# First self attention: one head at a time from memory, or two heads at a time from the projection's own tiles

## The chip, the cores and the metric

The program runs on one core of one Trainium2 chip, as one launch. The metric is device time in microseconds. TensorE multiplies matrices into PSUM, ScalarE evaluates functions, VectorE and GpSimd do elementwise work and reductions, SyncE only issues DMAs here. The engines run side by side and wait for each other through semaphores. Each engine takes its instructions in program order.

## The reference

Four layers of attention and feed-forward work on x (2 batches of 1024 tokens of 256). The change concerns the first attention alone:

```
q = l2norm(layer_norm(x) @ Wq) * q_scale            # 8 heads of 64
k, v = split(concat([layer_norm(x), layer_norm(ctx)]) @ Wkv); k = l2norm(k) * k_scale
sim = q . k * 8, masked where a context key is barred (keys 1024 to 1100)
out = softmax(sim) @ v
x = x + layer_norm(out @ Wo)
```

So there are 16 pairs of batch and head (B = 2, 8 heads), 1024 queries and 1101 keys each. The other stages (mixture of experts, two cross attentions, a second self attention, an fp4 feed-forward) are the same before and after.

## The kernel before

A stage is a block of code with buffers of its own; the next begins when all engines have ended. The first attention has three stages after its layer norm.

`project_normed` (stage qkv0) computes rows of q and k in 34 jobs: fp32 products into PSUM, squares on ScalarE, sums on VectorE, division by the length, transposition by TensorE, and a scaled copy into qT and kT, where two heads of 64 lie above each other in the 128 partitions. It ends with v (18 jobs). SyncE stores qT, kT and a row of mask values to device memory.

`head_attention` (stage heads0) takes 16 heads one after the other. BUFS = 4 sets of buffers are loaded from memory by SyncE (`load`, L1233 to L1257). For a head:
- `peak`: TensorE computes scores in bf16, queries in the partitions, 128 queries against 1101 keys (three products, L1307); VectorE takes the maximum of each query (`take_max`, L1420). Eight of these a head.
- `turn_max` (L1314), `copy_max` (L1431), `load_max` (L1263): the eight columns of maxima are transposed, copied and laid by DMA as row 64 of q, against a row of ones in k; row 65 holds the mask. This is done LEAD - 1 = 1 head ahead.
- `score` (L1332): 18 units (9 chunks of 128 keys by 2 halves of 512 queries), keys in the partitions, fp32, so that the maximum is taken off inside the product. ScalarE makes the exponential (L1408).
- `value` (L1344): the weighted sum of v, two chunks side by side in column tiles of 64.
- `add_weights` (L1458, VectorE) adds the nine chunks of exponentials; `fold` (L1320) transposes sums and weights, VectorE reduces (L1469, L1439) and multiplies by the inverse (L1446).

Which use of the shared PSUM comes after which score is written out by hand in USES and TIMES. The heads 4 to 11 run in a hardware loop, the first and last four are straight code. The PE order in a unit is score, value of an earlier group, and then what TIMES lists:

```
def score(n, u, i, j):
    ...
    pe.matmul(score_ps[0:rows, i % RING, :], k[:, u, c * P:c * P + rows], q[:, u, x:x + spec.unit],
              start=True, stop=True).then_inc(score_done, 1)
```

`output_rows` (stage out0, L1785 to L1875) packs the heads on GpSimd, transposes them (L1820), multiplies by Wo (L1808), and then normalises: one root over all 16 tiles after the last one, and whole-tile operations on VectorE.

`quad_attention`, the second self attention, is not changed. It already works with four heads of 16 at a time, with row tiles for the maximum rounds (L1638), fp32r scores (L1660) and column tiles for the sums (L1669). The cross attentions use row tiles of 32 with fp32 (L523).

Of the kernel before, what the change touches and what calls it, by code (L numbers as in the profile page):

```python
# [1096 lines left out]
def head_attention(nc, core, name, spec, q_dram, k_dram, mask_dram, values, out):  # L1097
# [5 lines left out]

    N, NU, HW, KEYS, QU = spec.n, spec.units, spec.width, spec.keys, spec.q_units
    W1 = HW + 1  # L1110
    BUFS, LEAD, LAG = 4, 2, 2
    SIDES = 4 if W1 <= 32 else 2
    SIDE = P // SIDES
    APART = SIDE < W1
    VW = HW if APART else W1
    ADDS = spec.chunks - 1
    GROUP = SIDES * QU
    GROUPS = -(-NU // GROUP)
    RING = 2 if spec.split else 3
    PROBS = 12 if APART else NU  # L1120
    assert BUFS * NU % PROBS == 0 and PROBS % QU == 0

    VALUE_TIMES = [list(range(QU))] if APART else [[x] for x in range(QU)]
    KEY_BANKS = -(-KEYS // 512)
    SHARED = 2 if KEY_BANKS == 2 else 1
    ROWS = 2 if spec.split else 1
    LOADS = 6 if spec.split else 5
    CF = KEYS // P

    TURN, FOLD, WEIGHTS = "turn", "fold", "weights"
    USES = [0, 1, TURN, 2] + ([WEIGHTS] if APART else []) + [3, FOLD] + list(range(4, BT))


    TIMES = [0, 2, 4, 5, 7, 9, 10, 12, 14, 16, 17] if APART else [0, 1, 3, 4, 6, 7, 9, 11, 12, 14]
    use_at = {k: [] for k in range(NU)}
    for time, x in zip(TIMES, USES, strict=True):
        use_at[time].append(x)
    assert SHARED == 1 or len(USES) % SHARED == 0  # L1140

    def exists(n, use):
        head = n + {TURN: LEAD - 1, FOLD: -1, WEIGHTS: -1}.get(use, LEAD)
        return 0 <= head < N

    uses_before, count = {}, LEAD * BT + LEAD - 1
    for n in range(N):
        for x in USES:
            uses_before[n, x] = count
            count += exists(n, x)  # L1150
    steady = uses_before[1, USES[0]] - len(USES)
    assert uses_before[N // 2, FOLD] == steady + len(USES) * (N // 2) + USES.index(FOLD)

    def before(n, use):

        return uses_before[n, use] if isinstance(n, int) else steady + len(USES) * n + USES.index(use)

    def buffer(n, use):
        return (uses_before[n, use] if isinstance(n, int) else steady + USES.index(use)) % SHARED

    with Stage(nc, name) as st:
        q = st.sb("q", [P, BUFS, S], spec.dtype)
        k = st.sb("k", [P, BUFS, KEYS], spec.dtype)
        narrow = not spec.split
        if narrow:
            q_peak = st.sb("q_peak", [P, BUFS, S], BF16)
            k_peak = st.sb("k_peak", [P, BUFS, KEYS], BF16)
        head_values = st.sb("head_values", [P, BUFS, spec.chunks, SIDE])
        minus_max = st.sb("minus_max", [P, BUFS, BT])
        max_rows = st.sb("max_rows", [BT, BUFS, ROWS, P], spec.dtype)  # L1170
        probs = st.sb("probs", [P, PROBS, spec.unit])
        sums = st.sb("sums", [P, 2, S])
        folded = st.sb("folded", [P, BT, VW])
        if APART:
            weights = st.sb("weights", [P, 2, S])
            added = st.sem("added")
        rsum = st.sb("rsum", [P, BT])
        shared_ps = st.ps("shared_ps", [P, SHARED, KEY_BANKS, 512])
        score_ps = st.ps("score_ps", [P, RING, spec.unit])
        sums_ps = st.ps("sums_ps", [P, S])  # L1180

        peaks = [shared_ps[:, x, :, :].rearrange("p a b -> p (a b)") for x in range(SHARED)]

        early = [peaks[0], score_ps[:].rearrange("p a b -> p (a b)")] if SHARED == 1 else peaks
        turned = [shared_ps[:, x, 0:2, :].rearrange("p a (t c) -> p a t c", t=4) for x in range(SHARED)]

        loaded = [st.sem(f"loaded{u}") for u in range(BUFS)]
        max_loaded = [st.sem(f"max_loaded{u}") for u in range(BUFS)]
        cleared, keys_cleared, narrowed = st.sem("cleared"), st.sem("keys_cleared"), st.sem("narrowed")
        shared_done, shared_read = st.sem("shared_done"), st.sem("shared_read")  # L1190
        high_done, max_ready = st.sem("high_done"), st.sem("max_ready")
        score_done, exp_done, value_done = st.sem("score_done"), st.sem("exp_done"), st.sem("value_done")
        sums_copied = st.sem("sums_copied")
        rsum_done, normed = st.sem("rsum_done"), st.sem("normed")
        n_keys_cleared = 4 if narrow else 2
        block = st.block()

        def at_least(eng, sem, value):

            if not (isinstance(value, int) and value <= 0):  # L1200
                eng.wait_ge(sem, value)

        def heads(eng, body):

            last = N // BUFS - 1
            for u in range(BUFS):
                body(u, u, 0)
            with eng.Fori(1, last) as j:
                for u in range(BUFS):
                    body(BUFS * j + u, u, j)  # L1210
            for u in range(BUFS):
                body(BUFS * last + u, u, last)

        def slot(u, i):

            return (NU * u + i) % PROBS

        def groups_upto(n, i):

            return GROUPS * n + i // GROUP + 1 if i >= 0 else GROUPS * (n - 1) + (i + NU) // GROUP + 1  # L1220

        def adds_upto(n, i):

            return ADDS * n + max(i // QU, 1) if i >= 0 else ADDS * (n - 1) + max((i + NU) // QU, 1)

        def beyond(n, ahead):

            return isinstance(n, int) and not 0 <= n + ahead < N

        @block.sync  # L1230
        def _(sp):
            def load(n, u):
                sp.dma_start(head_values[:, u, 0:CF, 0:VW].unsqueeze(1),  # L1233
                             values[:, bass.ds(n, 1), 0:CF, 0:VW]).then_inc(loaded[u], 16)
                if CF < spec.chunks:
                    rows = KEYS - CF * P
                    sp.dma_start(head_values[0:rows, u, CF:CF + 1, 0:VW].unsqueeze(1),
                                 values[0:rows, bass.ds(n, 1), CF:CF + 1, 0:VW]).then_inc(loaded[u], 16)
                if spec.split:

                    row = spec.peak_row
                    sp.dma_start(q[row:row + ROWS, u, :].bitcast(F32),
                                 q[row + ROWS:row + 2 * ROWS, u, :].bitcast(F32)).then_inc(loaded[u], 16)

                    for part in range(2):
                        src = q_dram[part, bass.ds(n, 1), :, :]
                        sp.dma_start(q[2 * part * HW:2 * (part + 1) * HW, u, :].bitcast(F32),
                                     src.to_broadcast([2, HW, S])).then_inc(loaded[u], 16)
                    for r in range(2):
                        src = k_dram[:, bass.ds(n, 1), :, :].rearrange("a o w s -> a (o w) s")  # L1250
                        sp.dma_start(k[2 * r * HW:2 * (r + 1) * HW, u, :].bitcast(F32), src).then_inc(loaded[u], 16)
                else:
                    sp.dma_start(q[0:HW, u, :], q_dram[0, bass.ds(n, 1), :, :].rearrange(
                        "o w s -> (o w) s")).then_inc(loaded[u], 16)
                    sp.dma_start(k[0:HW, u, :], k_dram[0, bass.ds(n, 1), :, :].rearrange(
                        "o w s -> (o w) s")).then_inc(loaded[u], 16)
                    sp.dma_start(k[HW:HW + 1, u, :], mask_dram[bass.ds(n, 1), :]).then_inc(loaded[u], 16)  # L1257

            def load_max(n, u):
                sp.wait_ge(max_ready, n + 1)  # L1260
                for r in range(ROWS):
                    row = spec.peak_row + r
                    sp.dma_start(q[row:row + 1, u, :].bitcast(F32),  # L1263
                                 max_rows[:, u, r, :].bitcast(F32)).then_inc(max_loaded[u], 16)

            sp.wait_ge(cleared, 3)
            sp.wait_ge(keys_cleared, n_keys_cleared)
            for n in range(BUFS):
                load(n, n)
            for n in range(LEAD - 1):  # L1270
                load_max(n, n)

            def body(n, u, j):
                if not beyond(n, LEAD - 1):
                    load_max(n + LEAD - 1, (u + LEAD - 1) % BUFS)
                if not beyond(n, BUFS - 1) and not beyond(n, -1):
                    sp.wait_ge(value_done, GROUPS * n)
                    load(n + BUFS - 1, (u - 1) % BUFS)

            heads(sp, body)  # L1280

# [1764 lines left out]
```

## Time and profile before

| | us |
|---|---|
| three runs, median (lowest to highest) | 3163.11 (3160.62 to 3172.48) |
| profiled execution, its own time | 3165.68 |
| span of its instructions | 3163.9 |

| engine | busy us, share of the span |
|---|---|
| TensorE (PE) | 2409.5, 76% |
| weight loads (PEld) | 1401.1, 44% |
| VectorE (DVE) | 1544.5, 49% |
| ScalarE (ACT) | 1126.9, 36% |
| GpSimd (POOL) | 347.7, 11% |

The shares are means over stages that have different limits, so the stages have to be looked at one by one. An fp32 product of the program stands as two matmul records. A busy TensorE says that records cover the time, not that it runs at its best speed: the granted clock (PEclk) stands beside it, 1.00 for 2.4 GHz and 0.50 for 1.2 GHz.

### The profile page before, as it was taken

What the parts mean: (1) busy time and instruction counts of PE and PEld (TensorE: products, weight loads), DVE (VectorE), ACT (ScalarE), POOL (GpSimd) and SP (SyncE); (2) the same over time, 40 slices, a digit from 0 to 9 for tenths busy, and PEclk for the clock granted to TensorE, in tenths of its full rate; (3) what the DMA queues carried; (4) which work ended last, traced back from release to release, by engine and by line L of the source; (5) the groups of instructions that cost most, each with busy time, mean ns of one, the idle gap of its engine ahead of it and who ended that gap; (6) DMA issues with size and microseconds to landing.
All of it is one profiled execution on the core that took longest, in us unless ns stands there. A gap on an engine that the chain in (4) does not pass through costs nothing. (4 is left out here: it accounts for less than half of the span.)

```text
span 3163.9 us, 38714 instructions
## 1 busy us (share of the span) xinstructions
PE 2409.5 (76%) x12273; PEld 1401.1 (44%) x12274; DVE 1544.5 (49%) x2425; ACT 1126.9 (36%) x2389; POOL 347.7 (11%) x369
## 2 busy tenths in 40 slices
PE   4959999998227587679999729996865999484487
PEld 2413333335117444323333319995333999331254
DVE  4657777763652354667786150002344000347665
ACT  3403333333103235126667424442432444233211
POOL 0010000001004201300000002221001222102211
PEclk9969999999558788759999959998786999686599
DMA  1220010100106300613342146663024666200001
GB/s 55 90 64 22 22 32 21 25 7 11 53 0 203 96 1 19 141 13 45 37 55 28 37 136 213 198 199 124 16 89 144 197 200 198 84 1 28 7 13 33
DMA packets 156570, 233.95 MB, mean 74 GB/s; under 512 B 48758, under 2 KB 110770, under 8 KB 156450
## 3 DMA queue, kind: packets, MB, share of 16 engines
q1 hardware_dynamic: 146754, 205.91, 23.8%
q0 software_dynamic: 9696, 26.49, 2.2%
q8 instruction: 69, 1.13, 0.2%
q14 instruction: 51, 0.42, 0.0%
HBM read 186.56 MB, written 38.86 MB: 71 GB/s over the span
## 5 line engine op out<-in xcount | busy, mean ns | idle before, releaser
L1721 DVE TENSOR_REDUCE heads_part_max<-heads_shared_ps 128x2 f32<-128x1024 f32 x256 | 300.0, 1220 | 90.1 <-PE heads_shared_ps L1638 90.1
L2759 PE MATMUL experts_up_ps<-experts_rowT,experts_w 128*128 128x128 f32 x2864 | 341.0, 277 | 0.0
L1705 ACT ACTIVATE heads_probs<-heads_score_ps 128x512 f32<-128x512 f32 x512 | 266.4, 602 | 191.0 <-PE heads_score_ps L1660 191.0
L2759 PEld LDWEIGHTS experts_up_ps<-experts_rowT,experts_w 128*128 128x128 f32 x2864 | 333.0, 194 | 0.2
L1408 ACT ACTIVATE heads_probs<-heads_score_ps 128x512 f32<-128x512 f32 (+1 forms) x288 | 171.9, 598 | 382.1 <-PE heads_score_ps L1332 380.3
L2909 DVE TENSOR_TENSOR experts_y<-experts_down_ps,experts_b_now 128x256 f32<-128x256 f32 x78 | 33.1, 425 | 555.6 <-PE experts_down_ps L2769 555.6
L1332 PE MATMUL heads_score_ps<-heads_q,heads_k 128*128 128x512 f32 (+1 forms) x576 | 291.6, 616 | 0.3 <-DVE heads_minus_max L1420 0.3
L2819 ACT ACTIVATE experts_hT<-experts_up_ps,experts_b_now 128x128 f32<-128x128 f32 x624 | 222.6, 368 | 46.5 <-PE experts_up_ps L2759 9.8
L1660 PE MATMUL heads_score_ps<-heads_q,heads_k 66*128 66x512 f32 x512 | 198.0, 474 | 29.5 <-ACT heads_probs L1705 25.3
L1420 DVE TENSOR_REDUCE heads_minus_max<-heads_shared_ps 128x1 f32<-128x1101 f32 x120 | 155.9, 1299 | 113.5 <-PE heads_shared_ps L1307 113.4
L2769 PE MATMUL experts_down_ps<-moe_w,experts_hT 128*128 x808 | 184.4, 379 | 0.0
L1660 PEld LDWEIGHTS heads_score_ps<-heads_q,heads_k 66*128 66x128 f32 x512 | 92.2, 201 | 198.4 <-ACT heads_probs L1705 163.5
L2769 PEld LDWEIGHTS experts_down_ps<-moe_w,experts_hT 128*128 128x128 f32 x808 | 148.9, 190 | 17.8
L1344 PE MATMUL heads_sums_ps<-heads_probs,heads_head_values 128*64 128x512 f32 (+1 forms) x576 | 154.6, 605 | 0.0
L1669 PE MATMUL heads_sums_ps<-heads_probs,self_values 128*32 128x512 f32 x1024 | 146.8, 647 | 4.1 <-ACT heads_sums L1697 4.1
L2708 POOL DMA_INDIRECT y_dram<-experts_y,experts_index x101 | 99.4, 985 | 454.3 <-DVE experts_y L2909 410.4
L2769 PE MATMUL experts_down_ps<-l1f_w,experts_hT 128*128 x624 | 141.0, 379 | 0.0
L1458 DVE TENSOR_TENSOR heads_weights<-heads_probs,heads_weights 128x1024 f32<-128x1024 f32 (+1 forms) x112 | 136.2, 1216 | 6.4 <-ACT heads_probs L1408 5.2
L1332 PEld LDWEIGHTS heads_score_ps<-heads_q,heads_k 128*128 128x128 f32 (+1 forms) x576 | 92.1, 187 | 92.4 <-issue 71.5
L2800 ACT ACTIVATE experts_rowT<-experts_rowT_ps 128x256 f32<-128x256 f32 x62 | 23.8, 384 | 296.4 <-PE experts_rowT_ps L2749 296.3
L2769 PEld LDWEIGHTS experts_down_ps<-l1f_w,experts_hT 128*128 128x128 f32 x624 | 115.7, 190 | 14.1
L1307 PE MATMUL heads_shared_ps<-heads_k_peak,heads_q_peak 128*128 128x512 bf16 x360 | 80.9, 335 | 40.7 <-DVE heads_k_peak L1480 26.0
(556 smaller groups left out, 3370.3 us busy)
## 6 DMA issues: line engine op xcount, KB each, us to landing
experts_w<-in_L_ffn_W SPq DMA_DIRECT2D x39, 1024.0 KB, 5.2
experts_w<-in_L_ffn_w SPq DMA_DIRECT2D x39, 1024.0 KB, 5.1
heads_q<-l_queries SPq DMA_DIRECT2D x48, 256.0 KB, 12.1
experts_w<-in_L_ffn_W SPq DMA_DIRECT2D x23, 512.0 KB, 3.9
core_xT<-y_dram SPq DMA_DIRECT2D x20, 512.0 KB, 4.7
experts_b_now<-in_L_ffn_b SPq DMA_DIRECT2D x78, 128.0 KB, 2.9
heads_k<-l_keys SPq DMA_DIRECT2D x32, 256.0 KB, 14.0
l1f_w<-in_L_ffn_W SPq DMA_DIRECT2D x8, 1024.0 KB, 11.9
```

The lines of the kernel that those rows point to most:

```text
L1332: pe.matmul(score_ps[0:rows, i % RING, :], k[:, u, c * P:c * P + rows], q[:, u, x:x + spec.unit], start=True, stop=True).then_inc(score_do ...
L1344: done = pe.matmul(sums_ps[x * SIDE:(x + 1) * SIDE, part * spec.unit:(part + 1) * spec.unit], head_values[0:rows, u, c, :], probs[0:rows, ...
L1408: act.activation(probs[0:rows, slot(u, i), :], score_ps[0:rows, i % RING, :], ACT.Exp, scale=spec.scale).then_inc(exp_done, 1)
L1420: dve.tensor_reduce(minus_max[:, u, s:s + 1], src[:, 0:KEYS], AX.X, ALU.max, negate=True).then_inc(shared_read, 1)
L1458: dve.tensor_tensor(total, chunk_probs(u, c)[0:rows, :], chunk_probs(u, 0) if c == 1 else total, ALU.add).then_inc(added, 1)
L1660: pe.matmul(score_ps[:, i % RING, :], k[:, u, r, c * P:(c + 1) * P], q[:, u, r, half * 512:(half + 1) * 512], start=True, stop=True).then_ ...
L1669: done = pe.matmul(sums_ps[r * SIDE:(r + 1) * SIDE, :], values[:, n, c, :], probs[:, t % SLOTS_OF_PROBS, r, :], start=(c == 0), stop=(c == ...
L1705: act.activation(probs[:, t % SLOTS_OF_PROBS, r, :], score_ps[:, i % RING, :], ACT.Exp, scale=SC).then_inc(exp_done, 1)
L1721: dve.tensor_reduce(part_max[:, g % 2, 2 * pair:2 * pair + 2, s, x], two, AX.X, ALU.max).then_inc(shared_read, 1)
L2759: done = pe.matmul(up_ps[:, f % 4, 0:SLOT], w1_sb[:, u, c, f * P:(f + 1) * P], rowT[:, u % 2, c, :], start=(c == 0), stop=(c == DC - 1))
L2769: done = pe.matmul(down_ps[:, u % 2, 0:D], hT[:, u % 2, f, :], second.sb[:, bass.ds(e, 1), f, :].rearrange("p o d -> p (o d)"), start=(f = ...
L2819: act.activation(hT[:, u % 2, f, :], up_ps[:, f % 4, 0:SLOT], func, bias=bias).then_inc(act_done, 1)
```

## The change

`head_attention` is replaced by `pair_attention`, `output_rows` by `output_normed` for this stage, and `project_normed` keeps its results on the chip.

- qT and kT stay in SBUF. GpSimd makes bf16 copies (q16, k16) during the projection. No store to memory, no loads of heads. Barred context keys are replaced in k16 by key 0 (six VectorE operations at the end of the projection), and the mask is the bias of the last chunk's exponential.
- A pair is the two heads of one 128-partition tile: 8 pairs, 18 steps each (2 halves by 9 chunks). A step's scores are two fp32 products of 64 rows, in row tiles 0 and 64, into two banks. Ahead of them two fp32r products of ones2 with max_rows put the negated maximum (as a high and a low part, two rows a head) into the same banks. One exponential covers both heads (1024 columns).
- Maximum rounds are a third of the keys (367 columns) of one head, in row tiles, three banks in a ring, three rounds in each step but steps 3 and 12. 48 rounds belong to a pair; 48 + 9 are done before the first step.
- The weights are added by VectorE (chunks 0, 2, 4, 8) and GpSimd (1, 3, 5, 6, 7) into two totals, merged by VectorE in the second step after the half. TensorE sums over the partitions by a product with ones (steps 3 and 12). SyncE lays the sums over 128 partitions, VectorE inverts them, SyncE stores and spreads them, and GpSimd scales the result in qT.
- Everything is straight code.
- `output_normed` needs no packing and no transposes; ScalarE copies the rows out, and statistics, roots and the last operations go in groups of four tiles; GpSimd adds the bias to x.

```
+    SLOTS_OF_PROBS, BANKS = 5, 3
+    BY_POOL = [1, 3, 5, 6, 7]
+    BY_VECTOR = [0, 2, 4, CHUNKS - 1]
+    NO_UNITS, TURN_AT, WEIGH_AT = (3, 12), 15, {3: 1, 12: 0}
+    LEAD = 9
...
+    work_at[-1] = units[0:UNITS] + [(TURN, 0)] + units[UNITS:UNITS + LEAD]
...
+        if s not in NO_UNITS and t < STEPS:
+            work_at[t] += left[0:3]
...
+            def load_max(g):                      # SyncE
+                sp.wait_ge(max_ready, g + 1)
+                for r in range(2):
+                    for part in range(2):
+                        row = HW * r + part
+                        sp.dma_start(max_rows[row:row + 1, g % 2, :].bitcast(F32),
+                                     max_parts[r * BT:(r + 1) * BT, part, :].bitcast(F32)).then_inc(max_loaded[g % 2], 16)
+            def invert(w):
+                sp.wait_ge(weights_copied, w + 1)
+                for r in range(2):
+                    sp.dma_start(compact[:, v, r, :], weights[HW * r:HW * r + 1, :]).then_inc(compact_loaded, 16)
+                sp.wait_ge(inverted, w + 1)
...
+                sp.dma_start(weights_dram[v, :, :]..., inverse[:, v, :, :]).then_inc(stored, 16)
+                sp.wait_ge(stored, 16 * (w + 1))
...
+                for r in range(2):
+                    sp.dma_start(spread[HW * r:HW * (r + 1), v, :], ...).then_inc(spread_loaded[v], 16)
+            for t in range(-1, STEPS + 4):
+                for item in work_at[t]:
+                    if item[0] == TURN:
+                        load_max(item[1])
+                    elif item[0] == WEIGH:
+                        invert(item[1])
...
+            def score(t):                         # TensorE
+                if t % PER == 0:
+                    pe.wait_ge(max_loaded[g % 2], 64 * (g // 2 + 1))
+                if t >= 2:
+                    pe.wait_ge(exp_done, t - 1)
+                for r in range(2):
+                    of = slice(HW * r, HW * (r + 1))
+                    pe.matmul(score_ps[0:rows, t % 2, r, :], ones2[of, 0:rows], max_rows[of, g % 2, half * 512:(half + 1) * 512],
+                              start=True, stop=False, tile_position=(HW * r, 0))
+                for r in range(2):
+                    of = slice(HW * r, HW * (r + 1))
+                    done = pe.matmul(score_ps[0:rows, t % 2, r, :], kT[of, c, b, chunk * P:chunk * P + rows],
+                                     qT[of, c, queries(t)[1]], start=False, stop=True, tile_position=(HW * r, 0))
+                done.then_inc(score_done, 1)
...
+            for t in range(STEPS):
+                score(t)
+                for item in work_at[t]:
+                    share(item)
+                if t:
+                    value(t - 1)
...
+            for t in range(STEPS + 4):            # VectorE
+                for item in work_at[t]:
+                    if item[0] != WEIGH:
+                        take(item)
+                if 1 <= t <= STEPS and (t - 1) % CHUNKS in BY_VECTOR[1:]:
+                    add(t - 1)
+                w = t // CHUNKS - 1
+                if t % CHUNKS == 2 and 0 <= w:
+                    merge(w)
+                if t % CHUNKS == 6 and 0 <= w and t < STEPS:
+                    invert(w)
+            invert(HALVES * PAIRS - 1)
```

`share` waits until the bank's last reader is done (`free`) and then makes a maximum round, the transposition of the maxima (TURN), or the product with ones (WEIGH). `value` makes two products of 64 columns, one a head, in column tiles. GpSimd takes its adds as the exponentials come, and `scale(w)` in the step of chunk 7 of the next half.

## Rows read from the trace of the kernel before

**Rows 1.** Windows: stretch; length, busy us (instructions) by engine; clock, DMA share, GB/s.
```profile
core 0: us, PE busy (x) PEld busy (x) DVE busy (x) ACT busy (x) POOL busy (x), PEclk, DMA share, GB/s
...
226.00:231.00 5.00, 4.86 (x8) 1.98 (x9) 2.51 (x2) 0.68 (x2) 0.00 (x0) 0.53 0.00 0
231.00:236.00 5.00, 5.00 (x18) 1.85 (x18) 1.58 (x2) 2.90 (x5) 0.00 (x0) 1.00 0.02 4
300.00:700.00 400.00, 388.70 (x1370) 144.35 (x1366) 288.16 (x276) 140.39 (x231) 0.00 (x0) 1.00 0.10 23
...
1376.00:1434.00 58.00, 58.00 (x200) 18.30 (x200) 30.02 (x27) 27.50 (x53) 0.00 (x0) 0.50 0.00 1
```

**Rows 2.** Timeline of SyncE's queue, one period: start us, us, engine, line.
```profile
397.60 0.72 SPq L1263 DMA_DIRECT2D heads_q<-heads_max_rows  x1
...
430.62 0.73 SPq L1263 DMA_DIRECT2D heads_q<-heads_max_rows  x1
```

**Rows 3.** Groups by line, 190 to 749 us: count, busy us, mean ns, idle before.
```profile
L1332 PE MATMUL heads_score_ps<-heads_q,heads_k 128*128 128x512 f32 (+1 forms) x576 | 291.6, 616 | 0.3 <-DVE heads_minus_max L1420 0.3
...
L1420 DVE TENSOR_REDUCE heads_minus_max<-heads_shared_ps 128x1 f32<-128x1101 f32 x120 | 155.9, 1299 | 113.5 <-PE heads_shared_ps L1307 113.4
L1344 PE MATMUL heads_sums_ps<-heads_probs,heads_head_values 128*64 128x512 f32 (+1 forms) x576 | 154.6, 605 | 0.0
L1458 DVE TENSOR_TENSOR heads_weights<-heads_probs,heads_weights 128x1024 f32<-128x1024 f32 (+1 forms) x112 | 136.2, 1216 | 6.4 <-ACT heads_probs L1408 5.2
...
L1320 PE MATMUL heads_shared_ps<-core_ident,heads_sums 128*128 128x128 f32 x128 | 17.2, 277 | 7.9 <-DVE heads_minus_max L1420 6.5 <-DVE heads_rsum L1469 1.4
```

**Rows 4.** Timeline of the output stage.
```profile
753.57 1.97 PE L1820 MATMUL out_turned_ps<-core_ident,out_packed 128*128 128x128 f32 x8 [6.94 <-DMA out_bias<-in_L_xattn_ln_o_b]
...
755.37 3.78 PE L1808 MATMUL out_row_ps<-out_w,out_headsT 128*128 128x256 f32 x8
...
808.54 4.42 DVE L1875 TENSOR_TENSOR core_x<-core_x,out_rows 128x4096 f32<-128x4096 f32 x1
```

**Rows 5.** Timeline at the seams of the three stages.
```profile
171.69 0.69 DVE L2194 COPY self_values<-qkv_v_ps 77x512 f32<-77x512 f32 x1 [1.03 <-PE qkv_v_ps L2101]
...
226.14 2.05 PE L1332 MATMUL heads_score_ps<-heads_q,heads_k 128*128 128x512 f32 x2 [0.28 <-DVE heads_minus_max L1420]
...
747.97 0.69 DVE L1446 TENSOR_TENSOR self_heads_out<-heads_folded,heads_rsum 128x512 f32<-128x512 f32 x1
...
749.15 0.44 SPq L1785 DMA_DIRECT2D out_w<-in_L_xattn_Wo  x1
```

**Rows 6.** The page's costliest groups: the second self attention's maximum.
```profile
L1721 DVE TENSOR_REDUCE heads_part_max<-heads_shared_ps 128x2 f32<-128x1024 f32 x256 | 300.0, 1220 | 90.1 <-PE heads_shared_ps L1638 90.1
```

**Rows 7.** Line L1613, the second self attention's loads of maximum rows.
```profile
DMA to landing us min/median/max: 2.1/2.1/2.2
```

**Rows 8.** Timeline of TensorE, tiled products of a cross attention and the second self attention.
```profile
2291.80 1.93 PE L523 MATMUL x_banks<-x_qT,x_k_half 32*77 32x512 f32 x8
2293.66 0.63 PE L529 MATMUL x_banks<-x_barredT,x_bar 77*77 77x512 bf16 x2
...
1507.10 0.49 PE L1660 MATMUL heads_score_ps<-heads_q,heads_k 66*128 66x512 f32 x1 [0.22 <-ACT heads_probs L1705]
1507.52 0.40 PE L1638 MATMUL heads_shared_ps<-self_k_narrow,self_q_narrow 32*128 32x512 bf16 x4
1507.85 1.06 PE L1669 MATMUL heads_sums_ps<-heads_probs,self_values 128*32 128x512 f32 x8
1508.84 0.96 PE L1660 MATMUL heads_score_ps<-heads_q,heads_k 66*128 66x512 f32 x3
```

**Rows 9.** The fp4 stage: timeline, then line L2246 with ns min/median/max.
```profile
2927.97 3.47 POOL L2241 TENSOR_TENSOR fp4w_rows_x<-fp4w_rows_x,fp4w_rows_power 128x1024 f32<-128x1024 f32 x1
2929.28 3.51 DVE L2246 TENSOR_TENSOR fp4w_raw<-fp4w_wide_x,fp4w_wide_scale 128x1280 f32<-128x1280 f32 x1
...
L2246 POOL TENSOR_TENSOR ffn_rows<-fp4w_rows_x,fp4w_rows_scale x4: 1930/2162/3059, 2913.5 to 2939.6; 128x1024 f32<-128x1024 f32 x4
L2246 DVE TENSOR_TENSOR fp4w_raw<-fp4w_wide_x,fp4w_wide_scale x2: 1492/2502/3511, 2929.3 to 2952.0; 128x1280 f32<-128x1280 f32 x2
```

More of the change, by code:

```diff
@@ L1230, in _ @@
         @block.sync
         def _(sp):
[L1232 to L1243, printed above, removed]
-                    for part in range(2):
[L1246 to L1271, printed above, removed]
@@ new lines, in scale @@
+            def scale(w):
+                v = w % 2
+                c, to = queries(w * CHUNKS)
+                pool.wait_ge(spread_loaded[v], 32 * (w // 2 + 1))
+                pool.wait_ge(sums_copied, w + 1)
+                pool.tensor_tensor(qT[:, c, to], qT[:, c, to], spread[:, v, :], ALU.mult).then_inc(scaled, 1)
+            for t in range(STEPS):
+                g, half, c = parts(t)
+                if c in BY_POOL[1:]:
+                    add(t)
+                if c == 7 and t >= CHUNKS:
+                    scale(t // CHUNKS - 1)
@@ L1386, in _, with free @@
-            heads(pe, body)
-            value(N - 1, BUFS - 1, GROUPS - 1, range(QU))
-            if APART:
-                pe.wait_ge(added, ADDS * N)
-                fold(weights, (BUFS - 1) % 2, count, 0)
-            pe.wait_ge(sums_copied, N)
-            fold(sums, (BUFS - 1) % 2, count + APART, (count + APART) % SHARED)
+            def free(used):
+                if used >= BANKS:
+                    reader, n = reads[used - BANKS]
+                    pe.wait_ge(weights_copied if reader == "scalar" else shared_read, n)
@@ new lines, in value @@
+            def value(t):
+                g, half, chunk = parts(t)
+                b, c = place(g)
+                rows = spec.chunk_rows(chunk)
+                pe.wait_ge(exp_done, t + 1)
+                if chunk == 0 and t:
+                    pe.wait_ge(sums_copied, t // CHUNKS)
+                for r in range(2):
+                    done = pe.matmul(sums_ps[HW * r:HW * (r + 1), :], values[0:rows, b * spec.heads + 2 * c + r, chunk, :],
+                                     probs[0:rows, t % SLOTS_OF_PROBS, r, :], start=(chunk == 0), stop=(chunk == CHUNKS - 1),
+                                     tile_position=(0, HW * r))
+                done.then_inc(value_done, 1)
```

675 lines of the change are left out of this document (349 added, 326 removed).

## The prediction

> **What bounds the kernel now.** I read the windows first. In the steady part of the first self attention (300 to 700 us) TensorE is busy 389 of 400 us at a granted clock of 1.00, its 2.4 GHz level, VectorE 288, ScalarE 140 [rows 1]. So this stage is TensorE's. The period of one head stands in SyncE's issues of the maximum row: 397.60 and 430.62, 33.0 us [rows 2], 16 heads, 528 us. The grouped lines say what fills it: score (L1332), weighted sum (L1344) and transposes (L1320) are fp32 products, while VectorE's maximum (L1420) and adding of weights (L1458) leave slack [rows 3]. One fp32 product of 512 columns costs 0.86 us at 2.4 GHz (four of 256 columns took 3.8 us at half clock, 0.45 each at full [rows 4]); a head has 18 for scores (15.5 us), 9 pairs for sums (7.7; two column tiles share one time), 16 transposes (2.1), 8 bf16 rounds for the maximum (3.7): 29 of 33 us. Ahead of the loop, VectorE's last copy of the projection starts at 171.69, the first score at 226.14; behind it lies a tail to 748.7, then an output stage from 749.15 to 813.0 [rows 4, 5].
>
> **Projection and start.** V's products keep TensorE busy to about 171, so the removed stores of q and k were covered and gain nothing. Added: six VectorE operations of 308 elements for the padded keys, some 0.46 us each with waits about 3.2 us, uncovered; two small mask loads, 0.5. GpSimd's bf16 copies lie beside TensorE. Then the clearing of big buffers, the loading of heads and the narrowing go (171.7+0.7 to about 198). New prologue: 1.8 us for max_rows and 0.8 for the ones; 57 reductions of 367 columns. A reduction costs 1.3 us for 1101 columns, 1.22 for 1024 [rows 3, 6]: 1.03 ns a column and 0.15 fixed, 0.55 us for 367, 0.51 apart when they queue (an estimate: they end up to 0.04 closer than they last). 48 x 0.51 = 24.5, reduce, transpose and two copies 1.9, four row loads: 4 x 0.72 issue, 2.1 to landing [rows 2, 7], 4.3 behind the first wait. The stage starts at 176.5, so the first score comes at 176.5 + 2.6 + 24.5 + 1.9 + 4.3 = 209.8, say 210.5 instead of 226.1: 15.6 gained. Bounds: 10 (SyncE late) to 20.
>
> **One step of the new loop** (two heads, one chunk, 512 queries; 18 steps a pair, 8 pairs), at 2.4 GHz.
> - Maximum by a product: 2 fp32r products side by side. Three fp32r products took 0.96 us, one 0.49: 0.235 apart [rows 8]. With the weight load 0.30.
> - Score: two fp32 products of 64 rows in row tiles. The nearest row is the mask attention's: four products of 32 rows in two pairs went from 2291.80 to 2293.66, 0.93 a pair, switch included [rows 8]. I take 0.88. If they don't overlap: 1.73.
> - Maximum rounds: three of 367 bf16 columns, 0.15 each by a column a cycle, neighbours in different row tiles; four tiles of 512 took 0.33 where one after another would be 0.85 [rows 8]. I take 0.31; 0.46 apart.
> - Sum: two column tiles, 0.86, plus 0.11 and 0.14 for the two changes of tile shape (0.33 for 0.21, 0.99 for 0.85 [rows 8]).
> Sum 2.6 us. A pair: 16 x 2.6 + 2 x 2.3 (steps without rounds) = 46.2, two ones products with waits for the merge 2 x 1.6 = 3.2, transpose 0.3: 49.7.
> VectorE a pair: 48 x 0.51 + 8 adds x 1.22 [rows 3] + small ones 2.2 = 36.5, below TensorE. ScalarE has the same exponentials as now, 140 us in 12.1 heads [rows 1], so 23. GpSimd 8 adds x 1.93 [rows 9] + 2 scalings = 17.6.
> Adding on two engines is not free. In the fp4 stage a GpSimd add of 1024 elements took 3.47 us where its fastest took 1.93, and the VectorE one beside it 3.51 instead of 1.49 [rows 9]: each waited the other out. Here VectorE's adds of chunks 2 and 4 come up about 3.1 us into their step, when GpSimd has just begun (2.7) on chunk 3 or 5: 1.5 us of waiting, 4 times a pair, VectorE 42.5. That still lies under TensorE, but a bank comes free late after chunk 4; I add 0.9 a pair: 50.6. From below 0, from above 8 full waits of 1.93, VectorE 52 with the rounds at 0.55, 54, so 3.4 more a pair.
> The Trainium skill (SBUF — State Buffer, "SBUF: two separate sides") says that the shared port pair is "an exclusive lock, not a bandwidth split", taken by a VectorE operation with two SBUF inputs only against a GpSimd operation that reads SBUF. The trace agrees on the lock, 3.51 against 1.49 [rows 9]. By that rule the reductions from PSUM are free of it; if it struck them too, 17.6 us of GpSimd would stand beside 24.5 of reductions, VectorE would reach some 50, and the time would be that of the second rival below.
>
> **The seam between pairs.** The first score of a pair waits for four loads of maximum rows. Their copy is placed in step 15, three steps or 7.8 us ahead. But in that step SyncE's queue still holds the inversion of the last weights: it waits for VectorE's reciprocal (behind three reductions and two copies, 4.3 us into step 15), stores (2.1 us to landing [rows 7]), waits for it, issues two spreads (1.5), and only then the four rows (2.2 to the last issue, 2.1 to landing). 4.3 + 0.1 + 2.1 + 0.1 + 1.5 + 2.2 + 2.1 + 0.2 = 12.6; 12.9 with half of a late add. TensorE stands still 5.1 us, and in order: rounds and the last sum are queued behind that score. Then the clock: it was at 0.50 when the old loop began, 0.53 over the first 5 us, 1.00 after [rows 1]. I charge 2.6 us a seam (about 5 us at half speed). 7 x 7.7 = 54. Bounds 0 and 7 x 10. 2.5 more for the loop's own start at half clock.
> Loop: 8 x 50.6 + 54 + 2.5 = 461.3, end at 671.8.
> Tail after the last exponential, all in a row: add and merge 2.6, ones product 1.3, copy 0.6, compaction 2.9, reciprocal 0.3, store 2.3, spread 3.8, scaling 1.0, with hand-overs 15.5 to 16.5. Stage ends at 688, before 748.7: 60.7 gained in all up to here.
>
> **Output stage.** Same load before the first product (749.15 to 753.57), then no transposes: 64 products of 256 columns x 0.43 = 27.5, half clock at the start 2.5 (the old one shows 3.78 for eight records [rows 4]), then of the last group copy, statistics, root, inverse and eight operations of 256, 5.5. 4.4 + 30 + 5.5 = 40 against 63.8: 23.5 gained (bounds 18 to 27). The whole-tile operations of 4.4 us at the old end, last at 808.54 [rows 4], are taken apart into groups beneath TensorE.
>
> Sum: 60.7 + 23.5 = 84. Later stages are untouched. The profiled span is 3163.9, its own time 3165.7, 2.6 above the median 3163.1. Median forecast 3163 - 84 = 3079.
>
> **Rivals.**
> 1. The seam is covered (landings quicker, or steps long enough that three of them last 12 us at no other cost): the 54 us go, 3025. For: SyncE's own waits are short when nothing is queued. Against: the order on SyncE is fixed and each landing is 2.1 us. 0.15.
> 2. The two adding engines bind: every VectorE add waits a whole GpSimd add. 8 x 3.4 = 27 more, with jitter 35: 3110. For: [rows 9]. Against: 45% load of GpSimd. 0.15.
> 3. The other side: row tiles of 64 rows with fp32 weights run one after the other. Place: score of each step; price 0.06 + 0.85 + 0.15, with the maximum product 0.24 more, 1.24 a step x 144 = 179; three steps then last 11.5 us, so the seam gives back 7 x 6.4 = 45: 3079 + 134 = 3213. It decides from 0.6 us a step (84 / 144). Against: rows of 32 do overlap [rows 8]. 0.05.
> 4. The clock stays at half. The later quad attention began with light rounds, then TensorE was busy 58 of 58 us at 0.50 [rows 1]. Against: its products fill 66 rows and 32 columns, the old loop's full ones brought 1.00 in 5 us, and here two tiles fill the array again. Throughout it would cost 2.2 us x 144 less the seams, 260: 3340; for the first pair alone, 20. 0.05 for the whole.
> Forecast 0.60, its own range 3050 to 3110.
>
> A measurement of this kernel tells about 0.5% (16 us) from no change. Faster: forecast, rivals 1 and 2, 0.90; same 0.02; slower 0.08 (rivals 3 and 4 less their mild forms, and mishaps). The range that leaves out at most 2 in 10: 3018 to 3150.
>
> **What would show it.** Score records of both heads starting within 0.1 us and a step of 2.6 us (else rival 3); a TensorE gap of 4 to 6 us before each pair's first score, ended by a DMA of max_rows, and clock 0.5 behind it (else rival 1); VectorE adds of 1.2 and of 2.5 to 3 us in the same loop; first score near 210; output stage of 40 us. Wrong would be: pair period far from 58 us, or windows of the loop at 0.5.

## The result, and the profile after

The changed kernel took 3027.3 us (median of 4, 3022.5 to 3037.7), the kernel before 3161.9 in runs beside it (3142.4 to 3172.5): ratio 0.959, 95% interval 0.953 to 0.964. That is 134.5 us where 84 were forecast: inside the range of 3018 to 3150, below the likeliest case's own range (3050 to 3110), and within 3 us of the time of rival 1 (3025). The profiled execution took 3037.7, span 3035.7; it answers to the 3165.7 of before, so the traces differ by 128 us. Where each stage stands in them, from views of the same kind:

| us | before | forecast | after |
|---|---|---|---|
| first score | 226.1 | 210.5 | 206.5 |
| first score to the end of the last exponential | | 461.3 | 428.8 |
| first score to stage end | 522.5 | 477.5 | 445.2 |
| output stage | 63.8 | 40 | 40.1 |
| SyncE's first moe_w load of the stage behind | 814.3 | | 693.6 |
| the remainder of the kernel (to the span's end) | 2349.6 | as before | 2342.1 |

120.7 us had been won when the stage behind the output begins. The other 7.5 are a matter of later stages, told of in the point on them below. (The profiled execution was the slowest of its four, so its 128 us lie under the 134.5 of the medians. In the second trace of the changed kernel, below, the remainder is 2330.1, 12 us shorter: later stages differ by that much between two executions of one kernel.)

The windows answer to [rows 1]: a plain stretch of the loop, then the seam between the first and the second pair in three pieces, then the last pair, and last the start of the second self attention.

```profile
core 0: us, PE busy (x) PEld busy (x) DVE busy (x) ACT busy (x) POOL busy (x), PEclk, DMA share, GB/s
240.00:249.70 9.70, 9.40 (x47) 3.00 (x43) 6.06 (x10) 3.89 (x5) 4.08 (x2) 1.00 0.02 2
249.70:251.90 2.20, 0.04 (x1) 0.00 (x0) 2.20 (x3) 0.81 (x1) 1.94 (x2) 1.00 0.00 0
251.90:256.40 4.50, 4.48 (x16) 1.40 (x16) 1.61 (x6) 0.23 (x1) 1.72 (x1) 0.62 0.03 1
256.40:261.00 4.60, 4.30 (x22) 1.39 (x23) 2.78 (x6) 1.91 (x2) 3.59 (x2) 1.00 0.32 61
1252.70:1267.70 15.00, 15.00 (x55) 4.79 (x53) 7.91 (x7) 8.15 (x16) 0.00 (x0) 0.50 0.00 1
```

TensorE's gap is 2.2 us, VectorE is busy all through it, and the granted clock behind it is 0.62. That is a mean of the two levels: the clock stands at 0.50, its 1.2 GHz level, for 3.4 of the 4.5 us (252.5 to 255.9) and at 1.00 for the rest. The timeline of the same seam (start, us, engine, line; in brackets the idle time before and who ended it) says who it was. First TensorE, step 15 of pair 0 from 248.08, then VectorE, then GpSimd, then SyncE.

```profile
248.08 0.50 PE L1295 MATMUL heads_score_ps<-heads_max_rows,heads_ones 64*128 64x512 f32 x2
248.41 1.02 PE L1299 MATMUL heads_score_ps<-self_qT,self_kT 64*128 64x512 f32 x4
249.27 0.47 PE L1272 MATMUL heads_shared_ps<-self_k,self_q 64*128 64x367 bf16 x3
251.92 0.28 PE L1276 MATMUL heads_shared_ps<-core_ident,heads_minus_max 128*16 128x128 f32 x1 [2.17 <-DVE heads_part_max L1382]
252.12 1.60 PE L1311 MATMUL heads_sums_ps<-heads_probs,self_values 128*64 128x512 f32 x4
...
254.25 1.87 PE L1299 MATMUL heads_score_ps<-self_qT,self_kT 64*128 64x512 f32 x4
...
260.31 0.50 PE L1295 MATMUL heads_score_ps<-heads_max_rows,heads_ones 64*128 64x512 f32 x2 [0.30 <-DMA heads_max_rows<-heads_max_parts]
```

```profile
248.49 0.20 DVE L1387 TENSOR_REDUCE heads_minus_max<-heads_part_max 128x16 f32<-128x48 f32 x1
248.61 2.80 DVE L1418 TENSOR_TENSOR core_xT<-core_xT,heads_probs 128x1024 f32<-128x1024 f32 x1
251.33 1.42 DVE L1382 TENSOR_REDUCE heads_part_max<-heads_shared_ps 128x1 f32<-128x367 f32 x3
```

```profile
247.98 2.35 POOL L1238 TENSOR_TENSOR core_xT<-core_xT,heads_probs 128x1024 f32<-128x1024 f32 x1 [3.76 <-ACT heads_probs L1363]
250.59 3.03 POOL L1238 TENSOR_TENSOR core_xT<-core_xT,heads_probs 128x1024 f32<-128x1024 f32 x1 [0.26 <-ACT heads_probs L1363]
```

```profile
253.63 0.40 SPq L1205 DMA_DIRECT2D heads_inverse_rows<-heads_inverse  x1
255.22 1.12 SPq L1210 DMA_DIRECT2D heads_spread<-heads_inverse_rows  x2
256.38 2.75 SPq L1194 DMA_DIRECT2D heads_max_rows<-heads_max_parts  x4
```

Read together: the three rounds of step 15 fill the three banks. VectorE can't empty one, for its add of chunk 4 started at 248.61, inside GpSimd's add of 247.98 to 250.33, and lasted 2.80 instead of 1.22. So the transpose, which needs a bank, goes 2.17 us late. Only then does SyncE's chain run, as the prediction has it; it ends with a wait of 0.30 us at the first score.

The groups by line over the loop (206 to 636 us) answer to [rows 3]: idle time before a group, with who ended it, is the last column.

```profile
L1295 PE MATMUL heads_score_ps<-heads_max_rows,heads_ones 64*128 64x512 f32 x256 | 67.4, 521 | 11.4 <-DMA heads_max_rows<-heads_max_parts 11.4
...
L1281 PE MATMUL heads_shared_ps<-core_xT,heads_ones 128*64 128x512 f32 x60 | 16.2, 611 | 3.8 <-DVE core_xT L1424 3.8
...
L1276 PE MATMUL heads_shared_ps<-core_ident,heads_minus_max 128*16 128x128 f32 x7 | 1.9, 277 | 13.0 <-DVE heads_part_max L1382 13.0
```

```profile
L1382 DVE TENSOR_REDUCE heads_part_max<-heads_shared_ps 128x1 f32<-128x367 f32 x329 | 156.5, 531 | 127.5 <-PE heads_shared_ps L1272 127.1
L1418 DVE TENSOR_TENSOR core_xT<-core_xT,heads_probs 128x1024 f32<-128x1024 f32 x16 | 43.4, 2715 | 8.4 <-ACT heads_probs L1363 8.4
...
L1418 DVE TENSOR_TENSOR core_xT<-heads_probs 128x1024 f32<-128x1024 f32 x16 | 19.5, 1220 | 12.2 <-ACT heads_probs L1363 12.2
```

The output stage, against [rows 4]: the products of line 1726, and the last group's last operations.

```profile
656.65 30.59 PE L1726 MATMUL out_row_ps<-out_w,self_qT 128*128 128x256 f32 x128 [15.41 <-DMA out_scale<-in_L_xattn_ln_o_w]
...
690.55 1.67 DVE L1771 SCALAR_TENSOR_TENSOR core_x<-out_rows,out_std,core_x 128x256 f32<-128x256 f32 x4
```

### The profile page after: what moved, and what is told of

Same layout as the page of the kernel before. It is cut to its first block and busy times, and to the rows that moved or that the text cites. A ratio compares the mean times of both kernels' runs of the same rounds, so it can differ in the third digit from the quotient of the medians.

```text
span 3035.7 us, 38003 instructions
## 1 busy us (share of the span) xinstructions
PE 2299.9 (76%) x12297; PEld 1336.9 (44%) x12298; DVE 1425.4 (47%) x2551; ACT 1093.3 (36%) x2264; POOL 542.5 (18%) x467
## 5 line engine op out<-in xcount | busy, mean ns | idle before, releaser
L1382 DVE TENSOR_REDUCE heads_part_max<-heads_shared_ps 128x1 f32<-128x367 f32 x384 | 181.1, 530 | 128.3 <-PE heads_shared_ps L1272 127.8
L2859 ACT ACTIVATE experts_hT<-experts_up_ps,experts_b_now 128x128 f32<-128x128 f32 x624 | 208.1, 367 | 83.0 <-PE experts_up_ps L2799 66.0
L1586 PE MATMUL heads_score_ps<-heads_q,heads_k 66*128 66x512 f32 x512 | 190.5, 455 | 31.5 <-ACT heads_probs L1631 27.3
L1363 ACT ACTIVATE heads_probs<-heads_score_ps 128x1024 f32<-128x1024 f32 x128 | 131.1, 1024 | 218.2 <-PE heads_score_ps L1299 215.7
L1311 PE MATMUL heads_sums_ps<-heads_probs,self_values 128*64 128x512 f32 (+1 forms) x576 | 158.9, 629 | 0.2 <-ACT heads_probs L1360 0.2
L1299 PE MATMUL heads_score_ps<-self_qT,self_kT 64*128 64x512 f32 (+1 forms) x576 | 155.9, 620 | 0.0
L1595 PE MATMUL heads_sums_ps<-heads_probs,self_values 128*32 128x512 f32 x1024 | 138.9, 615 | 4.3 <-ACT heads_sums L1623 4.3
L1238 POOL TENSOR_TENSOR core_xT<-core_xT,heads_probs 128x1024 f32<-128x1024 f32 x48 | 122.6, 2554 | 82.6 <-ACT heads_probs L1363 80.6
L2742 POOL DMA_INDIRECT experts_row<-rows_dram,experts_index x101 | 99.0, 980 | 81.1 <-DVE experts_index L2940 46.2
```

The costliest lines, as they stand in the source:

```text
L1238: pool.tensor_tensor(total, first, probs[:, t % SLOTS_OF_PROBS, :, :], ALU.add).then_inc(pool_added, 1)
L1299: done = pe.matmul(score_ps[0:rows, t % 2, r, :], kT[of, c, b, chunk * P:chunk * P + rows], qT[of, c, queries(t)[1]], start=False, stop=Tr ...
L1311: done = pe.matmul(sums_ps[HW * r:HW * (r + 1), :], values[0:rows, b * spec.heads + 2 * c + r, chunk, :], probs[0:rows, t % SLOTS_OF_PROBS ...
L1363: act.activation(probs[:, t % SLOTS_OF_PROBS, :, :], score_ps[:, t % 2, :, :], ACT.Exp, scale=SC).then_inc(exp_done, 1)
L1382: dve.tensor_reduce(part_max[:, g % 2, r, s, x:x + 1], bank[:, 0:PIECE], AX.X, ALU.max).then_inc(shared_read, 1)
L1586: pe.matmul(score_ps[:, i % RING, :], k[:, u, r, c * P:(c + 1) * P], q[:, u, r, half * 512:(half + 1) * 512], start=True, stop=True).then_ ...
```

## The experiments

Lines of the diffs are of `pair_attention`. "Loop" is from the first score to the end of the last exponential (the changed kernel's first trace: 428.8 us). First a control.

> The changed kernel once more, unedited, so that the edits beside it are compared with it on the same chip. Both theories: 3022 to 3038 us, the loop's first score to the last exponential 429 us, each of the seven seams between pairs 4 to 9 us over the plain steps.

Measured: 3027.3 us, loop 429.7, six seams like the first, one of 9 us. So a loop's length repeats to about 1 us between the two traces, and the kernel's median to 0.1 us.

**VectorE alone adds.**

```diff
-    BY_POOL = [1, 3, 5, 6, 7]
-    BY_VECTOR = [0, 2, 4, CHUNKS - 1]
+    BY_POOL = []
+    BY_VECTOR = list(range(CHUNKS))
...
-                if t % CHUNKS == 2 and 0 <= w:
-                    merge(w)
```

> VectorE adds all nine chunks of weights, GpSimd only scales; the merge goes. Theory A (the seam's stall stands at the transpose, which waits for a bank that VectorE gives back late because its add waited for GpSimd's): every add lasts 1.22 us, the gap before the transpose falls from 2.2 to below 1 us, the clock holds at the seams, loop 400 to 410 us instead of 429, kernel 20 to 28 us below the changed one. Theory B (the seam's stall is the row loads behind SyncE's inversion): the gap only moves to the first score and the clock still falls, loop within 8 us of 429. Rival to both (VectorE becomes the bound: 48 reductions 21.5 us, 16 adds 19.5, small ones 2 of a pair of 49.5, and 2.7 us in a step of 2.6): steps of 2.7 to 2.9 us, loop above 435.

Measured: 3033.3 us, ratio to before 0.960 (0.955 to 0.966), loop 428.3: no faster than the changed kernel, as theory B had forecast, and theory A's 400 to 410 failed. (The four runs lie at 3022.7, 3023.5, 3043.2 and 3044.0; the trace is the first.) The adds last 1.22 us, none waits for GpSimd. The wait at the transposes fell from 13.0 to 3.5 us, and the wait for the loads rose from 11.4 to 25.4. By line over the loop, then one seam:

```profile
L1295 PE MATMUL heads_score_ps<-heads_max_rows,heads_ones 64*128 64x512 f32 (+1 forms) x288 | 74.3, 511 | 25.4 <-DMA heads_max_rows<-heads_max_parts 25.4
...
L1276 PE MATMUL heads_shared_ps<-core_ident,heads_minus_max 128*16 128x128 f32 x7 | 1.9, 277 | 3.5 <-DVE heads_part_max L1382 3.5
```

```profile
254.19 1.08 PE L1311 MATMUL heads_sums_ps<-heads_probs,self_values 128*64 128x512 f32 x4
258.42 0.80 PE L1295 MATMUL heads_score_ps<-heads_max_rows,heads_ones 64*128 64x512 f32 x2 [3.15 <-DMA heads_max_rows<-heads_max_parts]
```

This seam is the one that was forecast: a gap before the pair's first score, ended by the DMA of the rows, at full clock until then. In the changed kernel it was hidden behind the wait at the transpose. VectorE as the bound is refuted too: steps of 2.61.

**GpSimd alone adds**, and the ones products read its sum.

```diff
-    BY_POOL = [1, 3, 5, 6, 7]
-    BY_VECTOR = [0, 2, 4, CHUNKS - 1]
+    BY_POOL = list(range(CHUNKS))
+    BY_VECTOR = []
...
-                if t % CHUNKS == 2 and 0 <= w:
-                    merge(w)
```

> GpSimd adds all nine chunks, VectorE only takes maxima; the merge goes. Theory A: VectorE is idle when a bank fills, so no wait at the transpose, no fall of the clock there, GpSimd at 8 x 2.36 + 1.27 = 20.1 us a half of 24.7; loop 400 to 405, kernel 25 to 30 us below the changed one. Theory B: loop within 8 us of 429, since SyncE's order is unchanged. Rival: GpSimd binds, because an add of 2.36 us in a step of 2.6 leaves no room for the scaling (1.3): probabilities' slots come free late once a half, loop above 435.

Measured: 3012.3 us, 0.952 (0.947 to 0.956), loop 415.6, 13 less than the changed kernel: about half of theory A's figure, and more than theory B's 8. The waits are 2.9 us at the transposes and 17.3 for the loads. Its adds last 2.34 to 2.38 us, none longer for VectorE, and it does not bind: steps stay at 2.61. Most of the 13 us are no gain at the seams; the step by step table below says where they are.

**The two products of a row tile issued together.**

```diff
                     pe.matmul(score_ps[...], ones2[of, 0:rows], max_rows[...], start=True, stop=False, ...)
-                for r in range(2):
-                    of = slice(HW * r, HW * (r + 1))
                     done = pe.matmul(score_ps[...], kT[...], qT[...], start=False, stop=True, ...)
```

> Same products, but both products of the first head's row tile are issued ahead of both of the second's, so that neighbours in TensorE's queue share a row tile. If only neighbours in different row tiles run side by side: the first head's fp32 product is alone, step 2.61 + 0.24 to 0.85 us, that is 3.1 to 3.5; 144 steps 70 to 125 us more, less some 20 given back at the seams: kernel 3080 to 3130. If the tiles run side by side in whatever order: step 2.6, kernel as the changed one. It also bounds what the serial case of the prediction would have cost.

Measured: 3024.9 us, loop 427.6, median step 2.62. The order makes no difference:

```profile
230.50 0.50 PE L1295 MATMUL heads_score_ps<-heads_max_rows,heads_ones 64*128 64x512 f32 x2
230.84 1.02 PE L1297 MATMUL heads_score_ps<-self_qT,self_kT 64*128 64x512 f32 x4
231.69 0.48 PE L1272 MATMUL heads_shared_ps<-self_k,self_q 64*128 64x367 bf16 x3
232.10 1.08 PE L1309 MATMUL heads_sums_ps<-heads_probs,self_values 77*64 77x512 f32 x4
```

Both L1295 products lie within 0.50 us, ahead of the L1297 of the first head, which stands between them in the program.

**Loads first on SyncE.**

```diff
                 for r in range(2):
                     sp.dma_start(compact[...], weights[...]).then_inc(compact_loaded, 16)
+
+            def store(w):
+                v = w % 2
                 sp.wait_ge(inverted, w + 1)
...
                         invert(item[1])
+                        if item[1] % 2 or item[1] == HALVES * PAIRS - 2:
+                            store(item[1])
+                    if item[0] == TURN and item[1]:
+                        store(HALVES * (item[1] - 1))
```

> SyncE issues a pair's four maximum-row loads ahead of the store and the two spreads of the inversion, which it had behind them; all else as in the changed kernel. Theory A (two waits in a row at a seam: first the transpose for a bank, 2.2 us, then the first score for the loads): the wait for the loads, 11.4 us over the seven seams, goes, the 13 us at the transposes stay and so does the fall of the clock behind them; loop 415 to 422 us instead of 429, kernel 5 to 15 us below the changed one. Theory B (SyncE's order is the seam's whole price, as the prediction had it): 7 x 5.7 = 40 us go, loop 390.

Measured: 3012.5 us, 0.953 (0.949 to 0.957), loop 410.6. The 13.0 us at the transposes stay, the wait for loads falls from 11.4 to 1.8. The kernel is 15 us faster, at the edge of theory A's range, and the loop, 18 us shorter, beyond it: what went with the wait for the loads was half clock as well. Theory B's price is refuted.

**Both waits taken away**: GpSimd alone adds, the loads go first, and GpSimd's scaling moved.

```diff
-                if c == 7 and t >= CHUNKS:
-                    scale(t // CHUNKS - 1)
+                if c == 0 and t >= 2 * CHUNKS:
+                    scale(t // CHUNKS - 2)
+            scale(HALVES * PAIRS - 2)
             scale(HALVES * PAIRS - 1)
```

> GpSimd alone adds, the loads go first on SyncE, and the scaling of a half moves from chunk 7 to chunk 0 of the half after the next, where GpSimd has no add. Theory A: both waits of the seam are gone (row copy ready at 10.4 us before the first score less 5.2, four issues 2.75, landing 2.1), the clock stays at 1.00 over the seams, pair period 50 to 51 us, loop 392 to 398, kernel 2988 to 3000. If only one of the two waits mattered: no faster than with GpSimd alone (loop 416).

Measured: 2982.2 us, 0.942 (0.938 to 0.946), loop 382.6: 46 us less than the changed kernel's, where GpSimd alone had given 13 and loads first 18. It has a third edit, the moved scaling; the kernel with VectorE alone and the loads first, below, does without it and comes to the same. One seam, then the loop as a window (clock 0.99):

```profile
247.56 0.47 PE L1281 MATMUL heads_shared_ps<-self_k,self_q 64*128 64x367 bf16 x3
248.51 0.28 PE L1285 MATMUL heads_shared_ps<-core_ident,heads_minus_max 128*16 128x128 f32 x1 [0.47 <-DVE heads_part_max L1391]
...
253.89 1.08 PE L1320 MATMUL heads_sums_ps<-heads_probs,self_values 128*64 128x512 f32 x4
254.90 0.50 PE L1304 MATMUL heads_score_ps<-heads_max_rows,heads_ones 64*128 64x512 f32 x2
```

```profile
206.00:588.00 382.00, 378.67 (x1828) 123.22 (x1830) 163.72 (x364) 166.72 (x175) 315.29 (x141) 0.99 0.05 12
```

The two ways of adding once more, both with the loads first (the first is the edit of VectorE alone with that of the loads, the second the kernel above unedited):

> VectorE alone adds and the row loads go first on SyncE. With VectorE alone and the old order on SyncE the loop took 428 us, as long as the changed one, its stall having moved from the transpose (13.0 to 3.5 us over the seams) to the loads (11.4 to 25.4). Theory A (two waits in a row, each able to hide the other's removal): now both are gone, pairs of 48.7 to 49.5 us, loop 383 to 390, kernel 2978 to 2992. Rival (VectorE is too full, 41 of 48.7 us, and gives the banks of step 15 back late once the seam no longer waits): transposes still wait 0.5 to 2 us each, the clock falls at some seams, loop 395 to 410.

> The kernel with GpSimd alone adding and the loads first, unedited, beside the one with VectorE alone on the same chip: 2977 to 2990 us as in its first runs, loop 383. If VectorE alone is as good in the loop it should be 2 to 4 us above it, since its tail was 12.8 us against 15.9.

Measured: 2988.6 us (0.943 to 0.947) with VectorE alone, loop 383.3; 2987.0 (0.941 to 0.948) with GpSimd alone, loop 382.7. The intervals overlap. The rival of a VectorE that is too full is refuted: it is busy 310 of 382 us, and the transposes wait 3.5 us in all. One adding engine is enough, and either of these is faster than both kernels.

**The loops step by step.** Each step's length is the time from the start of its maximum product (L1295 in the changed kernel) to that of the next step. Subtracted from it is the same step's length in the first trace of GpSimd alone with the loads first (loop 382.6), and the differences are added up by place; steps outside these places differ by less than 0.5 us in all.

| us over the loop | all | steps 3, 7 and 12 | seams (steps 15 to 17 and the next 0 to 2) |
|---|---|---|---|
| changed kernel | 46.2 | 10.2 | 35.5 |
| VectorE alone | 45.6 | 0.0 | 45.6 |
| GpSimd alone | 33.0 | 0.0 | 33.0 |
| loads first | 27.9 | 10.2 | 17.6 |
| VectorE alone, loads first | 0.7 | 0.0 | 0.6 |

Steps 3, 7 and 12 hold what the splitting of the adds costs away from the seams: the merge ahead of the ones products, and a bank that comes free late in step 7. The seams cost 5.1 us each in the changed kernel. So GpSimd alone gained 10.2 us from the end of the split and only 2.5 at the seams, and VectorE alone lost at the seams what it gained from the split. Of single cures only loads first helped the seams, by half; both together take the whole.

**One row tile for both heads**, in both loops of `score`:

```diff
-                    of = slice(HW * r, HW * (r + 1))
+                    of = slice(0, HW)
...
-                              ..., tile_position=(HW * r, 0))
+                              ..., tile_position=(0, 0))
```

> Leaves out the second head's scores: its two products are computed from the first head's rows and in its row tile, so that the four products of a step go through one row tile. It measures what side by side in row tiles is worth. Row tiles overlap fully in the changed kernel: step 2.61 + 0.24 + 0.85 = 3.7 us, loop 429 + 144 x 1.09 = 586 less 20 to 35 us that longer steps give back at the seams. If they overlapped only in part there: step under 3.4.

Measured (one run): 3274.1 us, loop 672.6. The step is 3.54 to 3.70 us at clock 1.00, near the 3.7 expected, but 6.77 to 7.08 at 0.50, and there it stayed for the first 89 us (step 12 of the first pair) and behind five of the seven seams:

```profile
220.00:293.00 73.00, 73.00 (x134) 23.79 (x134) 20.48 (x32) 11.95 (x12) 9.60 (x5) 0.50 0.00 0
293.00:325.00 32.00, 30.77 (x109) 11.21 (x107) 14.85 (x28) 8.57 (x10) 10.44 (x5) 0.95 0.05 9
```

In each of these six stretches the full clock came back at the end of the step that holds the ones products, 0.4 us before to 1.3 us behind it (the first such step is 287.0 to 295.2 us, the rise at 295.9), and not before. One run shows this, and nothing was run on its cause.

**The kernel before, again.**

> The kernel before, unedited, for a second trace. In its first trace the second self attention runs at granted clock 0.50 until 1435 us, 404 us from its first exponential to its last; in five traces of the changed kernel and its edits the clock rises some 40 us earlier and it takes 390. If the slow start belongs to the kernel before (as most of its times near 3167 beside single ones at 3142 suggest): 404 again and 3160 to 3172. If it is luck of an execution: 390 and near 3145.

Measured (one run): 3157.4 us. Neither: the second self attention took 394.8 us from first to last exponential, its clock rising some 30 us after its first score (60 in [rows 1]'s trace):

```profile
1371.00:1400.00 29.00, 28.96 (x100) 9.81 (x104) 14.14 (x12) 14.47 (x28) 0.00 (x0) 0.50 0.00 1
1400.00:1405.00 5.00, 4.99 (x24) 1.40 (x24) 3.22 (x3) 2.14 (x5) 0.00 (x0) 0.71 0.00 0
```

## Why the prediction was right or wrong, point by point

- **Projection and start: right, 4 us short.** 206.5 instead of 210.5. The 48 reductions took 21.5 us, 0.447 from start to start, not the 0.51 assumed; that is 3.0 of the 4.0.
- **The step: right.** 2.61 us against 2.6; maximum, score, rounds and sum take 0.34, 0.86, 0.40 and 1.01 us from start to start. Both heads' records start within 4 ns. Rival 3 and rival 4 fell. Two of the workings don't come out of their own terms: four products of 256 columns in 3.78 us at half clock [rows 4] are 0.47 each at full and 0.94 for 512 columns, not 0.86 (0.86 is what the trace after shows); and rival 3's 0.06 + 0.85 + 0.15 + 0.24 is 1.30 a step, not 1.24.
- **The pair: right in sum.** A plain pair is 50.3 us (13 steps of 2.61, and steps 3, 7, 8 and 12 of 3.52, 3.40, 2.56 and 3.52, and step 15 of 3.36, as it is with GpSimd alone adding), forecast 50.6. Its terms were off: step 15 is 0.75 longer than a plain one, where 0.3 was charged for the transpose. The transpose's own record is 0.28; 0.47 is TensorE's wait for the bank, which is there even with VectorE free of adds (the seam of GpSimd alone with the loads first, above). The lock was told as four waits of 1.5 us a pair; there are two (chunk 4: 2.72 against 1.22; chunk 2 got away). The split costs TensorE 0.8 us in step 7 (2.61 with one adding engine) and 0.4 in each of steps 3 and 12, where the ones product waits for the merge (3.15 there): 1.5 a pair against 0.9, 10.2 in the whole loop. By the Trainium skill (SBUF — State Buffer, "SBUF: two separate sides") a VectorE operation takes that lock when it has two SBUF inputs or runs in a two-port mode; a reduction from PSUM has one input and none in SBUF. The traces agree that it is free of the lock: 531 ns in the changed kernel, 533 beside a GpSimd that is busy 315 of 382 us, 532 beside one that is busy 20 (VectorE alone, loads first).
- **The last pair: a step missed.** It was priced like the others, but there is no maximum to take for a ninth pair. With both waits gone it takes 43.2 us (44.7 in the changed kernel, whose seam before it reaches into it), 7.4 less. For the same reason the last three steps of the seventh pair are 1.5 us shorter, and the first pair's step 3, which has no ones product yet, is 1.2 shorter.
- **The seam: the term that failed, mis-sized.** "TensorE stands still 5.1 us" plus "2.6 us a seam" for the clock, 54 in all; measured 35.5, 5.1 each, by the table of the loops step by step. Of them 29.4 lie in steps 15 to 17, 4.2 a seam against the 5.1 of the stall, and 6.1 behind two of the seven seams, 0.9 a seam against the clock's 2.6. Three steps of 7.8 us and SyncE's chain of 12.9 leave 5.1 in all, whatever fills them. In the changed kernel the stall came first at the transpose (13.0 us in seven), so the half clock behind it fell, at five of the seven seams, into the time that TensorE would have waited for the loads anyway. The prediction asked of the transpose only its 0.3 us, not who holds its bank. The chain's length, from step 15's start to the first score, was 12.2 to 13.2 us in six of seven, but in part by luck: in the seam shown, VectorE's reciprocal starts 5.3 us into step 15, not 4.3, and what follows takes 6.9, not 8.3. With GpSimd alone adding, where VectorE is on time, the chain is 10.5 to 11.4 in the first six.
- **Rival 1 was wrong, though its time was the measured one.** Nothing covers the seam: taking its two waits away gave 46 us more (loop 429 to 383, 10 of them the split's). The nearness of 3027 to 3025 is chance: smaller terms elsewhere added up to it. The prediction's own sign against the forecast, a pair period far from 58 us, would have pointed at neither: it is 54.9 on average. "A gap before the first score ended by a DMA" was shown by the trace only as a remnant, 0.3 us in the seam above.
- **Rival 2: refuted.** It had 27 to 35 us for adds that wait for each other; steps stayed at 2.61 and the split cost 10.2 in the loop. GpSimd alone, with 2.36 us for each of 16 adds a pair, does not bind either.
- **Tail and output stage: right.** 16.4 us against 16.2, and 40.1 against 40, 23.7 less than before.
- **"Later stages are untouched": right in code, wrong in time.** From the second self attention's projection norm to the norm behind it went 582.7 us, before 599.7; the stages after that gave 10 back, for which no run gives a cause. Of the 17 us 14.5 lie between first and last exponential, 389.8 against 404.3; there the clock rose 18 us after the first score instead of 60 [rows 1]. All ten traces with the new first attention have 390 us from first to last exponential there, the two of before 404 and 395. Why it rises when it does stays open; nothing was run on it.

By the traces, then: 4.0 start + 7.4 last pair + 18.5 seams + 6.2 small terms of the loop (its start 1.4, seven pairs 2.1, and 1.2 and 1.5 for what the first and the seventh pair lack) make 36 of the 36.5 us that the stage behind the output starts earlier than forecast (84.2 to 120.7), and later stages the rest.

## What to carry to other kernels

Waits that stand in a row on one engine hide each other: of 35.5 us at the seams, curing the wait at the transpose gave 2.5 (GpSimd alone) or less than nothing (VectorE alone), curing the wait for the loads 18, and both together all of it. So price a seam as the longest chain from its first hold to its end less the steps beside it, once, and don't add the whole of the clock's fall to a stall that it may fall into. Compare such edits step by step and not by the loop's length alone: here an edit meant for the seam gained most of its 13 us in other steps. Before splitting elementwise work between VectorE and GpSimd, see whether one of them has the room: here the split cost 10.2 us in the plain steps, and either engine alone none.

## What the runs showed of the hardware

- Products of different row tiles don't stand in the trace in the kernel's order: with (head 1: maximum, score; head 2: maximum, score) written, head 2's maximum product started 10 ns behind head 1's and 0.33 us ahead of head 1's score. The Trainium skill (TensorE: Matmul & The Clock Gate, "Part 3: Packing small matmuls — row/col tiling") has matmuls strictly first in, first out, in start and end; the starts in this trace disagree. Whether TensorE's queue changed the order or the compiler had done so before is not shown.
- With the scores of both heads in one row tile, TensorE was busy 73 of 73 us at 0.50 and did not rise; it rose each time at the end of the step in which the ones products and then the sum's, column tiles over all 128 rows, follow each other without a round between them. With the scores in two row tiles it was at 1.00 5.1 us behind the first score. So row tiles were worth more than their overlap here: 672.6 against 428.8 us, 244 more, where 144 steps of 1.09 make 157.
- GpSimd's fastest add of 1024 elements, 1.93 us in [rows 9], was no measure: with GpSimd alone adding it takes 2.36 here (mean of 96).
